# A state-space block with matmuls before the first input, and u x D written by ScalarE from the fourth group on

## The reference

```python
def step(h, inp):
    d, b, c, ut = inp
    dA = jnp.exp(d[:, :, None] * A)
    h = dA * h + (d * ut)[:, :, None] * b[:, None, :]
    y = jnp.einsum('bdn,bn->bd', h, c)
    return (h, y)
...
return ys.transpose(1, 0, 2) + u * D
```

## Time and profile before

| what | value |
|---|---|
| median of three runs | 1062.54 us (1056.73 to 1064.08) |
| profiled execution, its time | 1059.2 us |
| its span, first to last instruction | 1057.0 us |
| PE busy | 944.2 us (89%), 4320 instructions |
| DVE busy | 920.4 us (87%), 722 |
| POOL busy | 855.6 us (81%), 428 |
| ACT busy | 779.4 us (74%), 1241 |
| mean granted clock of PE | 0.953 |
| DMA traffic | 167.43 MB, 158 GB/s in the mean |

### The profile page before, as it was taken

How to read it: one execution, slowest core, us unless ns; L and a number is a source line. 1 busy time by engine, 2 the same in 40 slices (tenths; PEclk the granted TensorE clock), 3 DMA queues, 4 the chain that set the end, 5 groups by cost and what they waited for, 6 DMA issues and landing times.

```text
span 1057.0 us, 13719 instructions
## 1 busy us (share of the span) xinstructions
PE 944.2 (89%) x4320; PEld 603.2 (57%) x4320; DVE 920.4 (87%) x722; ACT 779.4 (74%) x1241; POOL 855.6 (81%) x428
## 2 busy tenths in 40 slices
PE   4698688879989999999999999989889987998897
PEld 3455456656645566555755575546655575556556
DVE  1988999999999999999999999898999999978701
ACT  4858767878598868987788869886687867777522
POOL 0777999989987998989897999899788898866400
PEclk9797699889999999999999999999999998999999
DMA  3855655673556645755456464664646564555100
GB/s 114 285 177 198 203 164 165 178 210 103 181 166 189 190 130 150 239 146 169 164 178 202 117 190 154 194 178 130 158 134 184 159 187 130 142 172 150 39 1 16
DMA packets 97670, 167.43 MB, mean 158 GB/s; under 512 B 9920, under 2 KB 33408, under 8 KB 97344
## 3 DMA queue, kind: packets, MB, share of 16 engines
q1 hardware_dynamic: 97600, 166.57, 52.6%
HBM read 159.19 MB, written 7.34 MB: 158 GB/s over the span
## 4 chain that ended last, share of the span: by engine, by line
PE 44%; ACT 17%; issue 16%; DVE 14%; POOL 8%; DMA 1%; SPq 0%; DVEq 0%; POOLq 0%; ACTq 0%
DVE bank_d L980 9%; PE bank_y L1274 9%; PE bank_m L1104 8%; PE bank_m L1180 7%; POOL state L595 5%; PE bank_m L1187 5%; ACT bank_d L745 4%; ACT L626 4%; PE bank_m L1153 3%; DVE state L978 2%; POOL state L600 2%; PE bank_m L1194 2%; PE bank_m L1162 2%; PE bank_m L1169 2%; PE bank_m L1122 1%
## 5 line engine op out<-in xcount | busy, mean ns | idle before, releaser
L595 POOL TENSOR_TENSOR state<-du,b_rows 128x1024 f32<-128x1024 f32 (+1 forms) x288 | 629.1, 2210 | 53.6 <-PE bank_y L1274 46.1
L980 DVE TENSOR_TENSOR_SCAN bank_d<-bank_d,state 128x1024 f32<-128x1024 f32 (+1 forms) x225 | 461.2, 2050 | 32.0 <-ACT bank_d L745 30.9
L745 ACT ACTIVATE bank_d<-delta,a_neg 128x512 f32<-128x512 f32 (+1 forms) x540 | 322.6, 634 | 78.2 <-DVE state L985 73.5
L1274 PEld LDWEIGHTS bank_y<-ident,state 128*128 128x128 f32 x2048 | 243.9, 147 | 92.5 <-issue 63.4
L1274 PE MATMUL bank_y<-ident,state 128*128 128x128 f32 x2048 | 270.2, 284 | 25.9 <-DVE gated L996 12.5
L985 DVE TENSOR_TENSOR state<-bank_d,c_rows 128x1024 f32<-128x1024 f32 (+1 forms) x225 | 248.8, 1106 | 7.7
L600 POOL TENSOR_TENSOR state<-state,c_rows 128x1024 f32<-128x1024 f32 (+1 forms) x63 | 134.1, 2128 | 16.7 <-DVE state L978 15.7
L1104 PE MATMUL bank_m<-xnT,w_conv 128*128 128x508 f32 (+7 forms) x288 | 118.4, 557 | 4.5 <-DVE x1T L1005 2.4
L1187 PE MATMUL bank_m<-hidA,h_s 128*128 128x512 f32 (+1 forms) x256 | 112.5, 585 | 5.7 <-ACT hidA L817 4.6
L1180 PE MATMUL bank_m<-hidB,h_s 128*128 128x512 f32 (+1 forms) x256 | 107.8, 573 | 0.8 <-DVE hidB L1019 0.8
L978 DVE TENSOR_TENSOR_SCAN state<-bank_d,state 128x1024 f32<-128x1024 f32 (+1 forms) x45 | 92.0, 2044 | 3.4 <-ACT bank_d L745 3.4
(11 more groups left out here) (152 smaller groups left out, 1047.6 us busy)
## 6 DMA issues: line engine op xcount, KB each, us to landing
b_rows<-bc_store SPq DMA_DIRECT2D x256, 256.0 KB, 5.0
c_rows<-bc_store SPq DMA_DIRECT2D x256, 256.0 KB, 4.7
wsel<-merged SPq DMA_DIRECT2D x32, 512.0 KB, 3.5
merged<-hidA SPq DMA_DIRECT2D x8, 512.0 KB, 3.1
h_s<-in_h SPq DMA_DIRECT2D x2, 1024.0 KB, 9.2
xin<-in_x SPq DMA_DIRECT2D x7, 256.0 KB, 5.1
out<-cT SPq DMA_DIRECT2D x7, 256.0 KB, 5.3
wsel<-in_factors SPq DMA_DIRECT2D x8, 160.0 KB, 3.5
```

Of the source, the lines that this page charges most:

```text
L595: nc.gpsimd.tensor_tensor(split(unit_state(u)), du[:, d, :, :width(g)], per_half(b_rows, u), ALU.mult).then_inc(S.bx_ready, 1)
L745: ins = act.activation(split(unit_decay(u))[:, h], delta[:, d, h, :width(g)], ACT.Exp, scale=a_neg[:, h, n:n + 1])
L980: dve.tensor_tensor_scan(decay, decay, drive, 0.0, ALU.mult, ALU.add).then_inc(S.scanned, 1)
L1274: ins = pe.matmul(bank_y[:, h, s * P:(s + 1) * P], split(unit_state(u))[:, h, s * LEN:(s + 1) * LEN], ident[:, :], start=(n == 0 and s == ...
```

## The change

It has four parts.

1. PE starts with `warm()`: once the identity is there, it multiplies it by itself 18 times into `bank_y`, which nobody reads.
2. `BY_SCALAR` falls from 7 to 3, so groups 3 to 6 now do what groups 7 and 8 did.
3. `shift` is computed by one POOL instruction for the group, right behind the reciprocal deviation; ACT's 128x1 instructions go away. `rstd` and `shift` are both POOL's now, and ACT waits for `shift` alone.
4. The start is ordered anew: the first two experts' merges come before the backward convolution of group 0; those fills and those of z are issued later; the table of the softplus is loaded ahead of the first dbc; delta and du of group 0 move by three units of the timeline, so that two merges stand ahead of them on DVE; and the six back matrices are loaded one by one between units 28 and 51, each with a semaphore.

```diff
-SETUP = {"fuse": -2.0, "wi0": -7.0, "wo0": 4.5, "wi1": -7.5, "wo1": 3.5, "wi2": 10.5, "wo2": 12.5, "wi3": 10.5,
+SETUP = {"fuse": -2.0, "wi0": -16, "wo0": -15.5, "wi1": -15, "wo1": -14.5, "wi2": 10.5, "wo2": 12.5, "wi3": 10.5,
...
+MERGED_FROM = -0.5
+WARMING = 18
+BACK = {"w_glu": 28.0, "w1": 33.0, "w2": 35.0, "h1": 39.0, "h2": 45.0, "w3": 51.0}
...
-BY_SCALAR = NG - 2
+BY_SCALAR = 3
...
-                if at == LOADS["back"]:
-                    load_back()
+                for name, dst, src, loaded in back:
+                    if at == BACK[name]:
+                        sp.dma_start(dst, src).then_inc(loaded, 16)
...
-                    if at == SETUP[f"wo{e}"] + MERGE_LAG + 0.5:
+                    if at == max(SETUP[f"wo{e}"] + MERGE_LAG + 0.5, MERGED_FROM + e):
...
                 nc.gpsimd.tensor_tensor(rstd[:, :n], var_eps[:, :n], half_power[:, :n], ALU.pow).then_inc(S.rstd_ready, 1)
+                pool.wait_ge(S.rstd_ready, g + 1)
+                nc.gpsimd.tensor_tensor(shift[:, :n], neg_mean[:, :n], rstd[:, :n], ALU.mult).then_inc(S.shift_ready, 1)
...
             def normalise(g):
-                act.wait_ge(S.rstd_ready, g + 1)
-                for t in range(sequences(g)):
-                    ins = act.activation(shift[:, t:t + 1], neg_mean[:, t:t + 1], ACT.Copy, scale=rstd[:, t:t + 1])
-                ins.then_inc(S.shift_ready, 1)
                 act.wait_ge(S.shift_ready, g + 1)
...
-                use_table(table_of(g, name))
+                use_table(EXP_LN if (g, name) == (0, "dbc0") else table_of(g, name))
...
+            def warm():
+
+                wait(pe, S.ident_ready, 1)
+                for i in range(WARMING):
+                    pe.matmul(bank_y[:, 0, 0:P], ident[:, :], ident[:, :], start=True, stop=True, skip_group_check=True)
+
+            warm()
```

More of the change, by code:

```diff
@@ L46 @@
 POOL_UNITS = (3, 8, 12, 17, 21, 26, 30)
-AHEAD, AHEAD_LEAD = (8, 17), 5
+AHEAD = (8, 17)
+AHEAD_LEAD = 5
 FILL = {"norm": -25.5, "uf0": -23.0, "uf1": -21.0, "ur0": -23.5, "ur1": -19.0, "z0": -18.5, "z1": -18.5, "dbc0": -9.5,
@@ L79 @@
 SUM_LAG, HELD = 2, 3
+WARMING = 18
 TURN = (19.0, 36.0)
 LOADS = {"x": -40.0, "bc_store": (-7.5, -1.0), "selected": (23.5, 26.5, 28.5, 31.0), "store": 76.0, "back": 3.0}
+BACK = {"w_glu": 28.0, "w1": 33.0, "w2": 35.0, "h1": 39.0, "h2": 45.0, "w3": 51.0}
 ROW_LEAD, C_LEAD = 6, 3
-FIRST_GROUP = {"ur1": 5.5, "h1_1": -2.0, "h2_0": 0.0, "power": -3.5, "bc_store": 1.0, "ur0": 10.0, "z0": 6.5, "z1": 8.5,
+FIRST_GROUP = {"ur1": 17.5, "h1_1": -2.0, "h2_0": 0.0, "power": -3.5, "bc_store": 1.0, "ur0": 21.0, "z0": 18.0, "z1": 18.5,
                "dbc0": -9.0, "dt00": -7.5, "dt01": -8.0, "dbc1": 7.5, "dt10": 7.5, "dt11": 7.0, "out": 0.0, "glu1": 1.0,
@@ L270, in build @@
         bank_m = [ctx.enter_context(nc.psum_tensor(f"bank_m{i}", [P, GT], F32)) for i in range(2)]
-        names = """small_loaded conv_loaded front_w_loaded fuse_w_loaded back_w_loaded factors_loaded0 factors_loaded1 base_loaded
+        names = """small_loaded conv_loaded front_w_loaded fuse_w_loaded glu_w_loaded w1_loaded w2_loaded h1_loaded h2_loaded w3_loaded factors_loaded0 factors_loaded1 base_loaded
             ident_zero ident_ready power_ready cols_ready rot_act rot_dve rot_ready a_ready conv_ready
@@ L512, in _ @@
             load_factors(1)
[L513 to L516, removed]
+            back = (("w_glu", w_glu_s[:, :], w_glu, S.glu_w_loaded), ("w1", w1_s[:, :], w1, S.w1_loaded),
+                    ("w2", w2_s[:, :], w2, S.w2_loaded), ("h1", h1_s[:, :, :], h1, S.h1_loaded),
+                    ("h2", h2_s[:, :, :], h2, S.h2_loaded), ("w3", w3_s[:, :, :], w3, S.w3_loaded))
             for at, groups in timeline():
@@ L1133, in fill_glu @@
             def fill_glu(g, m):
-                wait(pe, S.back_w_loaded, 6 * 16)
+                pe.wait_ge(S.glu_w_loaded, 16)
                 gy = rooms(g)[0]
@@ L1166, in fill_gate @@
             def fill_gate(g, f):
+                pe.wait_ge(S.w1_loaded, 16)
                 cT = rooms(g)[1]
@@ L1171, in fill_up @@
             def fill_up(g, f):
+                pe.wait_ge(S.w2_loaded, 16)
                 cT = rooms(g)[1]
@@ L1176, in fill_h1 @@
             def fill_h1(g, f):
+                pe.wait_ge(S.h1_loaded, 16)
                 hidB = rooms(g)[5]
@@ L1183, in fill_h2 @@
             def fill_h2(g, f):
+                pe.wait_ge(S.h2_loaded, 16)
                 hidA = rooms(g)[4]
@@ L1190, in fill_w3 @@
             def fill_w3(g):
+                pe.wait_ge(S.w3_loaded, 16)
                 hidB = rooms(g)[5]
```

## The result

The changed kernel takes 1086.3 us in the median of four runs (1076.0 to 1098.7), against 1060.5 us for the kernel before in four. The ratio is 1.0212, with a 95% interval from 1.0125 to 1.0298; in a second comparison it was 1.0227 (1.0186 to 1.0269). It is slower by some 2%, where the forecast, 1056 us, was a little faster. The longest of the four executions counts as slow and is left out of the ratio.

A forecast was written before the change was run, and what follows sets the result against it. The prediction took a chain of waits passing between ACT, PE and DVE as the bound. Its terms, -3.4 + 1.5 + 1.0 - 3.2 = -4.1 us, took 1059.2 to 1055.1; median put at 1056, range 1047 to 1066.

The forecast's parts named there:

- shift, -3.4 (0 to -5.3): ACT's four small instructions leave the chain, 0.75 us in each of 4.5 periods: -3.4 us.
- POOL is idle for 10 us of a period, which hides it: POOL's new shift instruction, 0.2 us a group, is hidden by idle time; without that cover, 1.6 us in all.
- u x D on PE, +1.5 (-6.9 to +3.4): Transposes ahead of gate in direction 0 cost +3.4 us; two matmuls gone in group 6's direction 1 give -1.9.
- rival B: PE is the bound everywhere, so u x D saves 6.9 us, shift 5.3, the start 3.2: 1045 us; chance 0.17.
- u x D on ACT, +1.0 (0 to +8.8): ACT's pair of writes takes 1.1 us: 0 in direction 0, some 0.25 left over four times in direction 1.
- the decays end 0.03 us before their scan: In both directions ACT's decays have 0.03 us before DVE's scan; without idle time each write pair costs 1.1 us.
- rival C: The writes of u x D stop DVE, each pair costing 1.1 us, +8.8 instead of +1.0: 1067.7 us; chance 0.11.
- PE is 0.75 us earlier by `shift`: In direction 0 DVE then waits only about 0.35 us for decays, against 0.71 saved at turn_y: 0.
- the sign given: In the profile after, DVE's wait at the first h1 take's scan, 1.02 us before, would be near 2.1 us.
- The start, -3.2 (0 to -4.5): At the start, the first convolution at high clock saves 2.8 us, the first transposes perhaps 0.2, shift 0.2.
- Rival A: PE's clock falls again before the first convolution, so the start gives only 0.3 us: 1058 us; chance 0.25.
- the fourth scan comes as long after the first convolution as before: At the start, the softplus table's 1.28 us gain is offset by merges and u_r and z copies: 0 (-1.3 to +1.0).

The follow-up runs named there:

- both placements mended: Changed kernel with the shift back on ScalarE and direction 0's u x D writes behind unit 16's decays in groups 3 to 6: 1062.2 us, ratio 1.0019.
- the shift alone and the pause: Kernel before with the shift on GpSimd, which also waits for its own previous drive before those of units 9, 10 and 11: 1058.0 us, ratio 1.0001.
- ScalarE's half alone: Kernel before with ScalarE also writing u x D from group 3 on, unread, while TensorE multiplies as before: 1072.2 us, ratio 1.0127.
- u x D alone: Kernel before with BY_SCALAR = 3 only, u x D written by ScalarE and summed by transposes: 1071.6 us, ratio 1.0117.
- second trace of the changed kernel: Changed kernel as it is, run again beside the kernels with GpSimd's added waits: 1085.2 us, ratio 1.0227; its profiled execution took 1089.5 us.
- the shift alone: Kernel before with only the LayerNorm's shift moved to one GpSimd instruction: 1072.6 us, ratio 1.0103.
- the shift backed out: Changed kernel with the shift back on ScalarE: 1075.7 us, ratio 1.0164.
- the added instruction: Kernel before, shift still on ScalarE, plus one short unused GpSimd multiplication of rstd by itself per group: 1079.4 us, ratio 1.0168.
- the start without the products: Kernel before with the changed kernel's start and loads only, without the 18 warm matmuls: 1062.9 us, ratio 1.0018.

## Why the prediction was wrong

Two steps failed that decide the time, and both put a term at nothing because of idle time elsewhere: that POOL's idle time hides the `shift`, and that the writes of u x D in direction 0 cost net 0 because PE is 0.75 us earlier. In their place the runs showed a lost turn of unit 8's scan, 7.2 us each, and 2.6 to 4.9 us in each direction 0. By the ratios of the edits alone the two cost 1.0% and 1.2%, and with both placements mended 0.2% is left.

**What bounds the kernel.** The reading that the chain goes round all the engines was right, and so was the warning that no share names the bound. It listed what DVE waits for, and overlooked what one instruction takes. The `early` scans of the kernel before took from 2.28 to 4.49 us for equal work, in a group whose mean was 2953 ns beside one of 2280. That row was the sign of the exclusion, and no term of the sum had it.

**shift, -3.4 (0 to -5.3).** The sizes were right: the GpSimd instruction takes 0.20 us, and PE's wait before glu is 0.61 us in the kernel with the shift alone and the pause, instead of 1.36, so gy is 0.75 earlier. The step that failed is "POOL is idle for 10 us of a period, which hides it". The idle time comes elsewhere. Ahead of unit 8 GpSimd's instructions follow one another, so 0.2 us move every boundary behind them, and alone the edit costs 1.03%. With the pause it is neutral, not -3.4. In the trace with the pause PE waits 1.04 us for `x1T` behind the next half of the convolution, where it did not wait before, since DVE, which makes `x1T`, is 0.43 us later by unit 8's scan:

```profile
492.62 3.66 PE L1104 MATMUL bank_m<-xnT,w_conv 128*128 128x512 f32 x8 [1.04 <-DVE x1T L1026]
```

An earlier gy only met the next limit. The count of 4.5 periods on a chain was not 4.5 times the saving.

**u x D on PE, +1.5 (-6.9 to +3.4).** Measured about 0 (0.9993, that is -3.0 to +1.4 us). The reasoning by place was right in that -6.9, rival B's term, did not come, and the wait for `turn_y` went as said.

**u x D on ACT, +1.0 (0 to +8.8).** Measured +13 with ScalarE's half alone (1.0127), outside the bounds. Three parts failed. The pair takes 1.32 us and not 1.1: the median of 604 ns in the earlier trace rows was a mean over two sizes, the wide form is 710. The step "PE is 0.75 us earlier by `shift`", which with the 0.71 us at `turn_y` made direction 0 come to 0, failed: the takes ahead of the pair did not come early enough, and all of 1.32 us reached DVE. And what was late next, unit 17's scan, was never named. The sentence "the decays end 0.03 us before their scan", which the prediction gave to rival C, was the one to build on. C is the rival that came closest, with its waits in direction 0. Its price was 1.1 us per pair; the true one is 2.6 to 4.9 in direction 0.

In direction 1 the sign given, a wait near 2.1 us after the take of h1_0, came at 4.18. In that stretch PE's h1 ran at half clock, 5.43 us for 4.28 before; windows and timeline of the changed kernel:

```profile
552.00:554.00 2.00, 2.00 (x6) 0.96 (x5) 1.97 (x2) 1.57 (x3) 1.58 (x2) 0.50 0.88 305
```

```profile
552.28 5.43 PE L1186 MATMUL bank_m<-hidB,h_s 128*128 128x512 f32 x8
```

In the kernel with u x D alone this wait is 2.48 us, with a shorter stretch at half clock, and with ScalarE's half alone, with no such stretch there, 0.32. The slower h1 accounts for 5.43 - 4.28 = 1.15 us of the wait. From gate to gate direction 1 costs 3.3 us in group 4 and 1.2 in group 3. What else makes it longer was not tested.

**The start, -3.2 (0 to -4.5).** Measured +2.5. Rival A's mechanism came: the granted clock falls while the first convolution runs, which takes 5.37 us and not 3.7. PE had stood idle for 3.5 us before. The rule that the Trainium skill gives (TensorE: Matmul & The Clock Gate, The HAM clock gate), that idleness brings the slow clock back, agrees with the trace, which shows 0.68 in the mean over the convolution, so a part of it at the lower level. Windows of the changed kernel over transposes and convolution:

```profile
11.60:12.70 1.10, 0.41 (x3) 0.20 (x3) 0.00 (x0) 0.56 (x1) 0.00 (x0) 1.00 0.00 0
12.70:18.10 5.40, 5.37 (x16) 4.15 (x16) 0.00 (x0) 0.47 (x1) 0.00 (x0) 0.68 0.00 0
```

The transposes gave their 0.25 us, the table load its 1.28, and the first scan comes at 28.74 us and not 31.06. The second comes at 33.85, for 33.52 before. The step "the fourth scan comes as long after the first convolution as before: 0 (-1.3 to +1.0)" is what failed: ACT waits 3.93 us for the u_r fill ahead of unit 1's decays, and that fill is at half clock behind the merges. The back matrices were hidden, as predicted; no engine waits for them.

**The groups 7 and 8** were not in the sum. The changed kernel loses 5.0 us between the two gates of group 7, with PE at half clock for 13.7 us from about 904 us on. A like stretch, with 3 to 5 us lost, stands in the second trace of the changed kernel and in those of ScalarE's half alone, the shift alone, the shift backed out, the added instruction and the start without the products, and not in those of u x D alone, both placements mended or the kernel before. What decides it was not tested.

## What to carry over

An instruction whose duration varies for equal work is a wait that no list of waits shows: look at minimum, median and maximum of each form before pricing anything. Where two engines exclude each other, a move of a few tenths of a microsecond on either can cost several microseconds, so a cost of nothing needs the two instructions that come to lie side by side, not the idle share of the period. Here GpSimd's idle time did not make its 0.2-us instruction free, since in the period shown none of that idle time lay between it and the drives beside unit 8's scan.

## What was not expected of the hardware

An excluded VectorE scan does not always get its turn at the next end of a GpSimd instruction. In groups 3 to 5 it was passed over at two ends in a row, and waited 5.1 us, while GpSimd had further instructions ready; it started when GpSimd paused for a semaphore. With a wait of GpSimd for its own previous result, at some 0.2 us, none of nine was passed over; the wait moves the ends too, so it isn't shown which of the two does it. The first ends that were lost lay 0.54 to 0.59 us behind the scan's start, read at the start of GpSimd's next instruction. At 0.33 us or less and at 1.2 us none was lost, but others at 0.55 to 0.61 were won, so the distance alone does not decide. In group 6 two more scans lost a turn (5.28 and 7.57 us), at 0.74 and 0.76. What decides is open.

In the start without the products, the granted clock reads 1.00 while the convolution takes 6.22 us; the same 16 instructions take 3.7 us at full clock. Windows of that kernel over the convolution (columns as in the earlier trace rows):

```profile
12.70:20.00 7.30, 6.22 (x16) 4.75 (x17) 0.00 (x0) 1.44 (x4) 0.00 (x0) 1.00 0.00 0
```

Before the first change of the clock its record is not to be trusted; the durations are.
